# The last layer's ternary weights quantised during the shared units, and combination, second gate and last feed-forward in one block

## The reference, cut to what matters

```python
x = x + xattn(ctx, layernorm(x), L0...)      # step 1: state space model, y * silu(layernorm(x)), transposed
x = x + moe(layernorm(x), ...)               # step 2: shared expert + 4 of 16 experts, weighted sum
x = x + xattn(ctx, layernorm(x), L1...)      # step 3: like step 1; y itself needs only ctx
x = x + ffn(layernorm(x), w_gate, w_up, w_down)   # step 4

def _quant_weight(w):
    scale = jnp.mean(jnp.abs(w)) + EPS
    return jnp.clip(jnp.round(w / scale), -1.0, 1.0), scale
def _quant_act(x):
    s = jnp.max(jnp.abs(x), axis=-1, keepdims=True) / 127.0 + EPS
    return jnp.clip(jnp.round(x / s), -128.0, 127.0), s
def _qlinear(x, w):
    wq, ws = _quant_weight(w); xq, xs = _quant_act(x)
    return jnp.einsum('bsi,oi->bso', xq, wq) * xs * ws
ffn: _qlinear(silu(_qlinear(x, w_gate)) * _qlinear(x, w_up), w_down)   # 512 -> 2048 -> 512
```

## Time and profile before

| | us |
|---|---|
| runs: median (lowest to highest) | 2203.43 (2201.49 to 2203.62) |
| the profiled execution's own time | 2204.01 |
| its span, first to last instruction | 2202.2 |
| VectorE busy in the span | 1747.1 (79%) |
| TensorE busy | 1621.7 (74%) |
| GpSimd busy | 1340.0 (61%) |
| ScalarE busy | 1160.9 (53%) |
| mean granted TensorE clock, share of 2.4 GHz | 0.885 |

### The profile page before, as it was taken

The page is one execution under the profiler, slowest core; times in us unless marked ns, Lnnn a source line. Parts: engine busy times, 40 slices in busy tenths (PEclk is TensorE's granted clock), DMA queues, the critical chain, the costliest instruction groups (busy, mean ns, idle before and its releaser), DMA issues. The chain is left out here.

```text
span 2202.2 us, 27001 instructions
## 1 busy us (share of the span) xinstructions
PE 1621.7 (74%) x8442; PEld 923.8 (42%) x8442; DVE 1747.1 (79%) x2274; ACT 1160.9 (53%) x1771; POOL 1340.0 (61%) x647
## 2 busy tenths in 40 slices
PE   4475666756647377889788899999999990006999
PEld 1121222212216145656566556665556660003554
DVE  2999999999965738996799668886488885856886
ACT  5676776766633025443544355554555550734776
POOL 2679878788953004993499528886178883752111
PEclk7788978889976589999999999999999995558999
DMA  7536546355645020001000433344434228540000
GB/s 260 197 132 211 194 155 215 132 189 184 189 168 225 3 72 6 15 8 38 11 11 1 164 105 137 144 164 153 164 121 155 85 71 314 175 152 6 20 25 29
DMA packets 110661, 264.10 MB, mean 120 GB/s; under 512 B 21664, under 2 KB 31264, under 8 KB 105312
## 3 DMA queue, kind: packets, MB, share of 16 engines
q1 hardware_dynamic: 77408, 183.72, 24.0%
q0 software_dynamic: 11520, 37.76, 5.8%
q10 hardware_dynamic: 21600, 40.90, 5.0%
HBM read 180.16 MB, written 82.18 MB: 119 GB/s over the span
## 5 line engine op out<-in xcount | busy, mean ns | idle before, releaser
L483 POOL TENSOR_TENSOR ssm_hs<-ssm_hs,ssm_Cs 128x1024 f32<-128x1024 f32 x128 | 314.0, 2463 | 88.2 <-DVE ssm_hs L450 88.2
L483 POOL TENSOR_TENSOR moe_hs<-moe_hs,moe_Cs 128x1024 f32<-128x1024 f32 x128 | 302.1, 2360 | 53.4 <-DVE moe_hs L450 52.4
L450 DVE TENSOR_TENSOR_SCAN moe_hs<-moe_dA,moe_bu 128x1024 f32<-128x1024 f32 x128 | 292.6, 2286 | 20.4 <-ACT moe_dA L364 12.2
L473 POOL TENSOR_TENSOR moe_U<-moe_U,moe_hs 128x1024 f32<-128x1024 f32 x128 | 301.7, 2357 | 6.5
L450 DVE TENSOR_TENSOR_SCAN ssm_hs<-ssm_dA,ssm_bu 128x1024 f32<-128x1024 f32 x128 | 291.7, 2279 | 0.1
L296 PE MATMUL ssm_pY<-ssm_hs,ssm_ident 128*128 128x512 f32 x512 | 276.3, 667 | 8.7 <-POOL ssm_hs L483 8.5
L1352 PE MATMUL moe_pgu<-moe_xsh,all_Wreg 128*128 128x256 f16 x1408 | 248.6, 275 | 1.9 <-DVE moe_hsl L1589 1.6
L1402 PE MATMUL moe_pgu<-all_Wreg,moe_xth 128*128 x1280 | 243.3, 312 | 0.0
L735 POOL TENSOR_TENSOR ssm_wlo<-ssm_wst,ssm_whi 128x1360 f16<-128x1360 f32 (+2 forms) x63 | 189.2, 3003 | 45.1 <-ACT ssm_wst L670 45.1
L364 ACT ACTIVATE ssm_dA<-ssm_dlt,ssm_A 128x511 f32<-128x511 f32 x256 | 167.9, 709 | 59.8 <-DVE ssm_hs L450 56.9
L1352 PE MATMUL moe_pgu<-moe_xsl,all_Wreg 128*128 128x256 f16 x704 | 193.6, 275 | 0.0
(11 more groups left out here) (264 smaller groups left out, 3431.4 us busy)
## 6 DMA issues: line engine op xcount, KB each, us to landing
ssm_wst<-in_w_all SPq DMA_DIRECT2D x51, 680.0 KB, 5.0
y_d<-moe_yo ACTq DMA_DIRECT2D x80, 256.0 KB, 2.7
all_Wreg<-w_hi SPq DMA_DIRECT2D x16, 1088.0 KB, 5.8
all_Wreg<-w_lo SPq DMA_DIRECT2D x16, 1088.0 KB, 9.0
w_hi<-ssm_whi SPq DMA_DIRECT2D x51, 340.0 KB, 2.3
w_lo<-ssm_wlo SPq DMA_DIRECT2D x51, 340.0 KB, 3.1
ssm_Cs<-c_d SPq DMA_DIRECT2D x64, 256.0 KB, 5.1
all_Wreg<-w_sh SPq DMA_DIRECT2D x11, 768.0 KB, 10.7
```

The source lines that it names most:

```text
L450: self.nc.vector.tensor_tensor_scan(self.hs[:, j, :, :].rearrange("p k t -> p (k t)"), self.dA[:, q, :, :].rearrange("p k t -> p (k t)"), ...
L473: self.nc.gpsimd.tensor_tensor(Y, Y, self.hs[:, j, :, :], ALU.add).then_inc(self.acc_done, 1)
L483: self.nc.gpsimd.tensor_tensor(self.hs[:, j, :, :], self.hs[:, j, :, :], self.Cs[:, i:i + 1, :].to_broadcast([P, HC, L]), ALU.mult)\
```

## The change

- **Weights.** Each ternary matrix is treated in 8 pieces of 128 x 1024, 24 in all, inside the shared units (`class Ternary`). ScalarE runs an absolute value with a summed output over each piece in slots 6 to 29 (`act_abs`), VectorE and TensorE form the three scales in slots 30 and 31, and from slot 33 each piece is loaded again and takes two ScalarE passes in alternate slots (`act_up`, `act_out`); ScalarE's queue stores it as bf16 to `wq_d` in DRAM. The pieces are staged in two buffers that belong to the expert steps (`yo` and `xt`), so nothing is added to the chip's memory. SP's loads of the shared token tiles are interleaved with the 48 piece loads.
- **Loading.** `Wreg`, the memory of the expert ring and the shared weights, now stays until the end, and takes in the token tiles of the shared units. When the shared units are done SP loads rows 5 to 9 of the rounded weights behind the ring, and rows 0 to 4, 10 and 11 into ring places as the last experts leave them.
- **One block.** `combine`, `gate` and `quant_ffn` become `tail`, with one start instead of three. The ring of gathers has 16 buffers. VectorE clips the twelve weight rows (bf16) in the first part. Combination and gate go sequence by sequence: tiles 0 to 3 (and 4, 5) come before the first tile of the last part, the rest stands between the groups of tiles 0 to 10. For each sequence there are two square roots of their own on ScalarE (`root`).
- Tile 0's xq is clipped on VectorE instead of GpSimd, and `layernorm(i + 2)` moves from group 2 to group 3.

```diff
+XSH = 2 * CSH * WC
+WQ = 2 * 2 * WE
...
+def last_row(r, j):
+    o = WQ + j * IF if j < 10 else (j - 10) * IF
+    return r["Wreg"][:, o:o + IF].bitcast(BF16)
...
+class Ternary:
+    N = 24
+    ABS, TOTAL, ROUNDS = 6, 30, 33
...
+    def sp_load(self, sp, j):
+        n, w = j % self.N, self.W[j % 2]
+        if 2 <= j < self.N + 2:
+            sp.wait_ge(self.abs_rdy, j - 1)
+        elif j >= 2:
+            sp.wait_ge(self.q_rdy, j - self.N - 1)
+        z, k, h = n // 8, n % 8 // 2, n % 2
+        if z == 2:
+            w = w.rearrange("p (k n) -> p k n", k=2)
+        sp.dma_start(w, self.src[z][:, k, h]).then_inc(self.w_in[j % 2], 16)
+    def act_abs(self, act, j):
+        act.wait_ge(self.w_in[j % 2], 16 * (j // 2 + 1))
+        if j:
+            act.wait_ge(self.abs_rdy, j)
+        self.nc.scalar.activation(self.q[:], self.W[j % 2], ACT.Abs,
+                                  accum_out=self.sum[:, j // 8, j % 8:j % 8 + 1]).then_inc(self.abs_rdy, 1)
+    def act_up(self, act, n):
+        j = self.N + n
+        act.wait_ge(self.w_in[j % 2], 16 * (j // 2 + 1))
...
+        w = self.W[j % 2]
+        self.nc.scalar.activation(w, w, ACT.Identity, bias=self.rnd[:, 0:1],
+                                  scale=self.inv[:, n // 8:n // 8 + 1]).then_inc(self.up_rdy, 1)
+    def act_out(self, act, n):
+        act.wait_ge(self.up_rdy, n + 1)
+        if n:
+            act.wait_ge(self.q_out, 16 * n)
+        self.nc.scalar.activation(self.q[:], self.W[n % 2], ACT.Identity, bias=self.rnd[:, 1:2]).then_inc(self.q_rdy, 1)
...
+        act.dma_start(self.r["wq_d"][z][:, k, h * IF // 2:(h + 1) * IF // 2], self.q[:]).then_inc(self.q_out, 16)
...
+        Q = Ternary(nc, m, d, r, [yo[:].rearrange("p g h -> p (g h)"),
+                                  xt[:].rearrange("p z g k n -> p (z g k n)").bitcast(F32)], px)
...
+                for i in range(4):
+                    load_shared(i)
+                Q.sp_load(sp, 0)
+                Q.sp_load(sp, 1)
+                for slot in range(NU):
+                    t, c = divmod(slot, CSH)
+                    if c in XT and 2 * (t + 2) + XT.index(c) < TT:
+                        load_shared(2 * (t + 2) + XT.index(c))
+                    n = Q.piece(slot, Q.ABS, 1)
+                    if n is not None:
+                        Q.sp_load(sp, n + 2)
+                    n = Q.piece(slot, Q.ROUNDS + 1, 2)
+                    if n is not None and n + 2 < Q.N:
+                        Q.sp_load(sp, Q.N + n + 2)
...
+                def last_weights(rows):
+                    for j in rows:
+                        sp.dma_start(last_row(r, j), r["wq_d"][j // 4][:, j % 4, :]).then_inc(r["wq_in"][j // 4], 16)
+                sp.wait_ge(Q.q_out, 16 * Q.N)
+                sp.wait_ge(s_dn, NU)
+                last_weights(range(5, 10))
+                for n, rows in ((E - 2, range(5)), (E - 1, range(10, 12))):
+                    f = sp.value_load(r["first"][0:1, n:n + 1], min_val=1, max_val=NSTEP)
+                    sp.wait_ge(y_rdy, f)
+                    last_weights(rows)
...
+                    n = Q.piece(slot, Q.ABS, 1)
+                    if n is not None:
+                        Q.act_abs(act, n)
+                    n = Q.piece(slot, Q.ROUNDS, 2)
+                    if n is not None:
+                        Q.act_up(act, n)
+                    n = Q.piece(slot, Q.ROUNDS + 1, 2)
+                    if n is not None:
+                        Q.act_out(act, n)
...
-                def magnitude(n):
-                    dve.wait_ge(w_in[n], 16)
-                    V.tensor_reduce(wsum[:, n // 4, n % 4:n % 4 + 1], W[:, n, :], AX.X, ALU.add,
-                                    apply_absolute_value=True).then_inc(abs_rdy, 1)
...
-                def clip(n):
-                    dve.wait_ge(up_rdy, n + 1)
-                    V.tensor_scalar(W[:, n, :], W[:, n, :], ROUND + 1.0, ROUND - 1.0, ALU.min, ALU.max).then_inc(clip_rdy, 1)
-                for g in range(TT * TOPK):
-                    i, k = g // TOPK, g % TOPK
-                    dve.wait_ge(got[g % NR], 16 * (g // NR + 1))
-                    if k:
-                        dve.wait_ge(used, g)
-                    V.scalar_tensor_tensor(out=X[:, i, :], in0=yr[:, g % NR, :], scalar=r["w8"][:, i, k:k + 1],
-                                           in1=X[:, i, :], op0=ALU.mult, op1=ALU.add).then_inc(used, 1)
-                    if 1 <= g <= NP:
-                        magnitude(g - 1)
-                    if g == NP:
-                        total()
-                    if g == NP + 2:
-                        scales()
-                    if NP + 4 <= g < 4 * NP + 4 and g % 3 == 1:
-                        clip((g - NP - 4) // 3)
+        COMBINED = {0: (6, 7), 1: (8,), 2: (9,), 3: (10, 11), 4: (12,), 5: (13,), 6: (14,), 7: (15,)}
+        FETCHED = {0: (9,), 1: (10, 11), 2: (12,), 3: (13,), 4: (14,), 5: (15,)}
+        GATED = {(1, 2): 0, (1, 3): 1, (2, 0): 2, (2, 1): 3}
+        def gate_at(b, t, f):
+            first = (1, 0) if b == 0 else (0, 2)
+            if b + 1 < B and t == first[0] and 0 <= f - first[1] < 2:
+                return [(b + 1) * KC + 2 * (f - first[1]) + j for j in range(2)]
+            return []
+        def root_at(b, t, f):
+            return b + 1 < B and (t, f) == ((0, 3) if b == 0 else (0, 1))
...
+                sp.dma_start(ident_f[:], d["ident"]).then_inc(loaded, 16)
+                load_y(0)
+                sp.wait_ge(used, KC * TOPK)
+                load_y(1)
+                for b in range(2, B):
+                    sp.wait_ge(tr_rdy, KC * (b - 1))
+                    load_y(b)
+                    for i in range(KC * (b - 2), KC * (b - 1)):
+                        sp.wait_ge(x_rdy, i + 1)
+                        sp.dma_start(out[i * P:(i + 1) * P, :], X[:, i, :]).then_inc(o_out, 16)
...
+                def fetch(i):
+                    for k in range(TOPK):
+                        g = i * TOPK + k
+                        if g >= NR:
+                            pool.wait_ge(used, g - NR + 1)
+                        nc.gpsimd.indirect_dma_start(
+                            out=yr[g % NR], out_offset=None, in_=r["y_d"],
+                            in_offset=bass.IndirectOffsetOnAxis(ap=r["pos"][:, i, k:k + 1], axis=0)).then_inc(got[g % NR], 16)
+                def y_gate(i):
+                    b, t = divmod(i, KC)
+                    if t == 0:
+                        pool.wait_ge(y_in[b], 16)
+                    pool.wait_ge(g_rdy, i + 1)
+                    y = Y[:, b % 2, t, :]
+                    nc.gpsimd.tensor_tensor(y, y, G[:, b % 2, t, :], ALU.mult).then_inc(yg_rdy, 1)
+                def x_clip(i):
+                    pool.wait_ge(xr_rdy, i + 1)
+                    if i >= 2:
+                        pool.wait_ge(tx_rdy, i - 1)
+                    nc.gpsimd.tensor_scalar(xq[:, i % 2, :], xn[:, i % 2, :], -ROUND, 127.0, ALU.add,
+                                            ALU.min).then_inc(xq_rdy, 1)
+                for i in range(KC + 1):
+                    fetch(i)
+                for i in range(KC):
+                    y_gate(i)
+                for i in range(KC + 1, 2 * KC + 1):
+                    fetch(i)
+                for i in range(TT):
+                    b, t = divmod(i, KC)
+                    if i + 1 < TT:
+                        x_clip(i + 1)
+                    for f in range(FC):
+                        for j in gate_at(b, t, f):
+                            y_gate(j)
+                    for j in FETCHED.get(i, ()):
+                        fetch(j)
...
+                def clip(j):
+                    if j % 4 == 0:
+                        dve.wait_ge(r["wq_in"][j // 4], 64)
+                    V.tensor_scalar(Wq[j // 4][j % 4], Wq[j // 4][j % 4], 1.0, -1.0, ALU.min, ALU.max).then_inc(clipped, 1)
+                def weighted(i, k):
+                    g = i * TOPK + k
+                    dve.wait_ge(got[g % NR], 16 * (g // NR + 1))
+                    if k:
+                        dve.wait_ge(used, g)
+                    V.scalar_tensor_tensor(out=X[:, i, :], in0=yr[g % NR], scalar=r["w8"][:, i, k:k + 1],
+                                           in1=X[:, i, :], op0=ALU.mult, op1=ALU.add).then_inc(used, 1)
+                def combined(i):
+                    dve.wait_ge(used, (i + 1) * TOPK)
+                    V.bn_stats(st[:, 0, i, :], X[:, i, :]).then_inc(c_st, 1)
+                    dve.wait_ge(c_st, i + 1)
+                    V.bn_aggr(mv[:, 0, i, :], st[:, 0, i, :]).then_inc(c_mv, 1)
...
+                def gated(i):
+                    dve.wait_ge(tr_rdy, i + 1)
+                    V.tensor_tensor(X[:, i, :], X[:, i, :], y_bank(i)[:].rearrange("p k t -> p (k t)"), ALU.add).then_inc(xa_rdy, 1)
+                    dve.wait_ge(xa_rdy, i + 1)
+                    V.bn_stats(st[:, 1, i, :], X[:, i, :]).then_inc(a_st, 1)
+                    dve.wait_ge(a_st, i + 1)
```

(74 more changed lines are left out.)

338 lines of the change are left out of this document (142 added, 196 removed).

## The result

| | before | after |
|---|---|---|
| median (lowest to highest), us | 2203.52 (2201.49 to 2204.71) | 2142.84 (2140.37 to 2147.24) |
| profiled execution, own time / span | 2204.01 / 2202.2 | 2147.24 / 2145.4 |
| VectorE / TensorE / ScalarE / GpSimd busy in the span | 79 / 74 / 53 / 61% | 80 / 76 / 56 / 62% |

The ratio is 0.973 (95% interval 0.9714 to 0.9746): 2.7% faster. The forecast was 2167; 37.1 us of span were to be saved and 56.8 were. I read the profile after in the order of the prediction's terms.

A forecast was written before the change was run, and what follows sets the result against it. VectorE was busiest in the shared units and TensorE bounded the last part; in the new loop VectorE takes over. Sum -66.4 + 12 + 5 + 11.5 + 0.8 = -37.1 us, time about 2167 us, range 2140 to 2190.

The forecast's parts named there:

- rival 2: Contention, TensorE's clock and the prologue part of the shared units' cost are hidden: 2137 to 2149 us; chance 0.14.
- D: Tail: VectorE's weighted additions held up by GpSimd's xq clips and gate products, +12 us, ends 0 and 25.
- E: Loop of the tail: TensorE, no longer busy all the time, gets a lower clock, +5 us, ends 0 and 20.
- F: Shared units: the added quantisation work, mainly 72 ScalarE passes, shows as +11.5 us, ends 3 and 25.
- A: Head of the tail, up to the first product of tile 0, paced by the gathers: 52.3 us.
- B: Fifteen tile periods of the tail's loop, tiles 0 to 10 lengthened by VectorE's work: 233.7 us, before 172.8.
- C: End of the tail, behind the last tile's first product: 18.6 us, unchanged.
- clears: More semaphores to clear, some 15: +0.8 us at most.
- rival 3: TensorE's clock falls and stays down through tiles 0 to 10: +47 us, 2214, slower; chance 0.05.
- rival 4: Twelve table loads in the loop each cost 1.4 us of restart: +16.6 us, 2184; chance 0.04.
- rival 1: Contention and shared units' cost near their upper ends, 20 us each: 2183 to 2187 us; chance 0.15.
- rival 5: No gain: the head is as long as combination and gate were, needing 90 us; chance 0.02.

The follow-up runs named there:

- run 6: Changed kernel with the transposes and additions of group 1's second gate one step later (tiles 1 and 2): 2147.30 us, ratio 0.9757.
- run 9: Changed kernel with second roots behind step 3's silu, a one-column activation fetching the silu table, and group 1's second gate one step later: 2139.64 us, ratio 0.9719.
- run 11: The changed kernel measured once more, unchanged: 2148.65 us, ratio 0.9749.
- run 3: Changed kernel with three useless one-operand GpSimd operations more per tile in tiles 0 to 7: 2150.13 us, ratio 0.9766.
- run 4: Changed kernel with four useless two-operand GpSimd operations more per tile in tiles 0 to 7: 2161.10 us, ratio 0.9818.
- run 7: Changed kernel with 360 useless small TensorE matmuls in the head, 300 before the second gate's transposes and 60 behind: 2166.09 us, ratio 0.9837.
- run 12: Changed kernel with 300 useless small TensorE matmuls ahead of tile 12, where no gathers run: 2158.60 us in a single execution.
- run 2: Changed kernel without the quantisation beside the shared units (loads, ScalarE passes, stores and scales left out): 2138.53 us, ratio 0.9714.

## Why the prediction was right, and where its sizes were off

Direction and mechanism held (the loop gets longer since VectorE takes TensorE's place as its bound, and by less than the shorter way to its first product saves), and the time fell in the range. But 2143 is outside the 2150 to 2180 to which I gave 0.60, and what came is nearest to rival 2 (hidden, 2137 to 2149), whose terms D and E did cost next to nothing; the prologue part of F and the silu waits, which it also wanted hidden, were not. Term by term, profiled execution:

| term | forecast | measured |
|---|---|---|
| A head | 52.3 | 52.7 |
| B fifteen periods | 233.7 | 233.6, and 3 in tile 0 |
| C end | 18.6 | 18.6 |
| D VectorE against GpSimd | +12 | in B |
| E TensorE's clock | +5 | in B, 0 to 3 |
| F shared units | +11.5 | 7.0, and 1.7 of clock |
| clears | +0.8 | 0.1 (idle ahead of the stage 12.78, before 12.65) |
| start of the shared units | 0 | -1.6, scatter |

**A** held link by link: gathers at 1.4, the bf16 clips at 0.72 us mean hidden between them, one table load on the path.

**B** held as a sum, partly by errors that cancel. Too low was tile 1 (21.8, not 18.6): I had costed the gate products as VectorE's delay, not as a wait of TensorE, whose transposes stand ahead of its own next matmuls; runs 6 and 9 took it away and tile 1 went to 17.4. The others came 0.1 to 1.2 us shorter, from tile 2 to tile 10, but for 7 and 9. The three waits behind the second root were 2.37 each (forecast 2.5). All stops in tiles 0 to 10 were put at 16.4 us (187.6 less the 171.2 of VectorE's own chain); run 11 has 17.9 in waits over 0.5 us. Two signs of the prediction read otherwise: VectorE was busy 83% and not over 90%, and it was idle 33 us, where over 15 was named as a sign of being wrong. That bound did not fit the forecast itself, whose stops alone are more.

**D is the step that failed, at 12 us the largest part of the miss.** "The xq clip ... exposed 1.2 in each of eight tiles = 10" rested on a row of two-operand operations on both engines and carried it over to a clip that reads one tensor. Runs 3 and 4 part the two: one-operand work leaves the additions at 0.79, two-operand work makes them 1.41. What is left are the gate products: two additions of 1.58 in tile 1, 1.7 us. Had the clip been a two-operand operation, the estimate would have been of the right order: 45 us of such work cost 12.7, 10.5 of it in the additions.

**E** named nearly the right clock (0.88 over tiles 0 to 7 where I said 0.85) and too high a price: in the tiles that VectorE bounds it costs nothing, in tiles 1, 4 and 8 half a us to 1.3 where it falls further (run 7's table). As the fifteen periods of run 11 are 233.6 with the clock as it is, D and E together are worth 0 beside my 17, or B's base was too high by what they cost; the sum does not part these two.

**F** was right in place, high in size. The second prologue took 2.1 and the first 1.0 where I had 6 for both, the slots with transpose and copy of C 3.5 instead of 4.5, the scales 0.4 instead of 1. By the difference of two kernels with the passes (469.3) and without (463.9 - 1.7 = 462.2) it is 7.1.

**Rivals.** 3 (clock under 0.67) is out: 0.73 in tile 0 and about 0.9 after it. 4 is out: loads of 1.28, the silu starts at their end (1942.18 + 1.28, 1943.47 in the changed kernel). The Trainium skill, ScalarE: Activation LUTs, section "What ACT_TABLE_LOAD costs", adds a drain to each; no switch in these traces shows one. 1 is out with D and F. 5 is out with the head of 52.7.

The median lies 4.4 us under the profiled execution, more than the 1.8 around a span. What varies is ahead of the tail: its start moved over 10 us among kernels that are alike up to there, and 7.9 of these are there already at the first shared unit. Why is not settled.

## What to carry to other kernels

When an engine is laid under another's stage, cost first the engine's own chain and the waits where a third engine must deliver a whole group; here these sums came to within 0.4 us, though errors of 3 us in single tiles cancelled, and the surcharges for contention and clock were what erred. Before charging VectorE for a neighbour on GpSimd, look how many tensors the neighbour's operation reads. A table switch is best put where the waiting engine has more work than root and load take, and the load back can be fetched by an activation of one column in ScalarE's own idle time; here this won 2.2 us in tiles 6 and 7, and in tile 10 another wait took its place.

## What the runs showed of the hardware

**Beside gathers TensorE's short instructions come in bursts.** The small matmuls of run 7, timeline of TensorE beside the head's gathers, then busy time (columns as in the earlier trace rows):

```profile
1839.24 6.43 PE L2150 MATMUL ffn_pd<-ffn_ident 128*128 128x128 bf16 x70 [13.80 <-DMA ffn_ident_f<-in_ident]
1846.46 0.33 PE L2150 MATMUL ffn_pd<-ffn_ident 128*128 128x128 bf16 x3 [0.80 <-issue]
...
1858.19 0.37 PE L2150 MATMUL ffn_pd<-ffn_ident 128*128 128x128 bf16 x2 [0.96 <-issue]
1858.90 0.26 PE L2150 MATMUL ffn_pd<-ffn_ident 128*128 128x128 bf16 x1 [0.34 <-issue]
...
1865.31 10.37 PE L2150 MATMUL ffn_pd<-ffn_ident 128*128 128x128 bf16 x157 [1.05 <-issue]
```
```profile
1846.00:1865.00 19.00, 8.27 (x58) 4.62 (x59) 17.02 (x31) 2.24 (x3) 14.30 (x13) 0.63 0.68 195
1865.00:1876.00 11.00, 10.37 (x157) 10.10 (x157) 4.62 (x5) 3.76 (x6) 9.50 (x8) 0.86 0.46 154
1876.00:1893.00 17.00, 6.31 (x30) 3.94 (x31) 0.00 (x0) 0.00 (x0) 11.34 (x12) 0.57 0.72 209
```

The first 70 ran without a gap, though gathers were being issued from 1836.51 on; then 58 took 19 us, in bursts of one to six (once nine) that began 0.7 or 1.4 us apart, with "issue" as the reason. 157 ran in 10.4 us: they began with GpSimd's products (1865.30 to 1870.71), when no gather was issued, and went on for 4.8 us after the gathers had resumed at 1870.86; then the pace fell again. The bursts so follow the gathers with some delay. In run 12, without gathers:

```profile
2083.84 16.91 PE L2159 MATMUL ffn_py<-ffn_ident 128*128 128x128 bf16 x300
```

The head lost 21.4 us: the gate's sixteen f32 transposes began 10.0 us later, behind the small matmuls, came in pieces themselves, from 1881.14 to 1893.38 (12.2 us, where the changed kernel takes 3.6 in one piece from 1872.66 on), and the rest of the head took 2.8 more. So TensorE should not be given hundreds of short instructions beside a stream of indirect gathers. What it is in the gathers' stage that does it, no run here shows: run 12 leaves out the gathers, but also what else runs in the head. The unexplained 3 us of tile 0 in the changed kernel, also beside gathers, may be of this kind: its reason reads "remote", and nothing here settles it.

**A GpSimd operation that reads one tensor hardly holds up VectorE's two-operand additions; one that reads two does** (0.79 against 1.41 us, runs 3 and 4). **The clock can dip for 3.4 us even inside a stage at full clock**, behind a pause of TensorE of 2.6 to 3.2 us (0.74 over 6.5 us in run 2), and costs 1.7 us there.
